# Causal attention: diagonal maxima by mask rows, all maxima in two halves of TensorE's array, a fixed cyclic order, three operand buffers

## The chip, the cores and the metric

The kernel runs on one core of a Trainium2 chip. Its engines are TensorE (PE in the profile; PEld is its weight loader), VectorE (DVE), ScalarE (ACT), GpSimdE (POOL) and SyncE, whose queue (SPq) issues nearly all DMAs. The metric is the device time of one execution in microseconds (us), as the median of several runs. Less is better.

## The reference

Two transformer blocks on `x` of shape (16, 1024, 256), in FP32. What matters here is the attention of the second block: 16 heads of 16 dimensions over 1024 positions, causal, with a linear position bias (ALiBi), for each of 16 batch entries. It is cut here to its core:

```python
q = (x @ q_w + q_b).reshape(Bx, Tx, NH, HD).transpose(0, 2, 1, 3)
kv = (x @ kv_w + kv_b).reshape(Bx, Tx, 2, NH, HD).transpose(2, 0, 3, 1, 4)
k, v = (kv[0], kv[1])
att = jnp.einsum('bhqd,bhkd->bhqk', q, k) * (1.0 / np.sqrt(HD))
att = att + build_alibi_bias(NH, Tx)[None]
att = jnp.where(causal[None, None], att, -jnp.inf)
att = jax.nn.softmax(att, axis=-1)
y = jnp.einsum('bhqk,bhkd->bhqd', att, v)
y = y.transpose(0, 2, 1, 3).reshape(Bx, Tx, Cx)
return y @ o_w + o_b
```

## The kernel before

Three stages follow each other. `prepare` sets up constants and small products (to about 152 us), `project` makes q, k, v and the feed-forward part in 32 steps and stores them to DRAM (to about 870 us), and `attend` does the attention (the rest). The change is in `attend`, with small additions to the other two.

`attend` works through 64 tasks `t` (`GROUPS`): batch entry `t // 4` and group `t % 4` of four heads. q and k are held as sums of three BF16 parts, and their products of parts stand in one contraction of up to 109 rows: three position rows, six products of 16 dimensions (`NSLOT`, 99 rows to `KA`), three rows that subtract the row maximum (to `KB`, 102), and seven mask rows (to `KM`, 109). For each task PE does:

- `max` (30 units, L1499 to L1508): q times k for the keys before the diagonal block, into one of three PSUM banks `t_a`, and DVE reduces each bank to row maxima (L1647);
- `diag` (8 units, L1510 to L1518): the 128 x 128 diagonal blocks of four heads into a bank of the ring `t_r`; ACT copies it to `t_near` (L1608), POOL masks later keys there (L1750), and DVE reduces two blocks at once (L1654);
- `join` (DVE) and `split` (POOL) make three BF16 parts of the maxima, `rows` (L1525) turns them on PE, `lift` (ACT, L1616) copies them out, and SP writes them to DRAM (L1461), waits until they have landed, and reads them back into rows of `t_q` (L1463);
- `exp` (38 pieces, L1542 to L1557): logits with the maximum already subtracted, into the ring of four banks; ACT takes the exponential into one of six slots of `t_prob` (L1599), and POOL zeroes later keys in diagonal blocks (L1744);
- `weigh` (12 quads, L1559 to L1573): probabilities times v in FP32, four heads side by side in column tiles of 32, into the bank `t_y`;
- `swap`, `invert`, `scale`, `back` on DVE (L1668 to L1688) turn and divide the result; `yhigh` (ACT) and `ylow` (POOL) split it, and for each fourth task PE does four units `out` (L1528 to L1540), which DVE adds to the residual (L1693).

The order of the instructions on each engine is fixed before the run. `plan()` (L1177) walks through time with given costs and picks, for PE, the unit of lowest rank whose inputs would be ready; the orders of the other engines follow. Operands `t_q`, `t_k`, `t_v` have four buffers, one for each group of heads; the 13 loads of task t + 4 are issued by SP after the last `weigh` of task t (L1465).

Of the kernel before, what the change touches and what calls it, by code (L numbers as in the profile page):

```python
# [11 lines left out]
P = 128  # L12
# [10 lines left out]
GH = 4  # L23
# [13 lines left out]
SUB = 16  # L37
EPS = 1e-5
# [3 lines left out]
class Chain:  # L42
# [5 lines left out]
    def __call__(self, ins):  # L48
        self.n += 1
        ins.then_inc(self.sem, 1)  # L50
        self.eng.wait_ge(self.sem, self.base + self.n)


def prepare(nc, a, scr):
# [8 lines left out]
    with ctx:  # L63
# [18 lines left out]
        keep(early, "t_v0", [P, QT, VPAD])  # L82
        blocks = keep(early, "t_blocks", [KM - KB, P])
        blockb = keep(early, "t_blockb", [KM - KB, P], BF16)
        for name in ("t_s_c0", "t_s_qkv0"):
            scr[name] = early.enter_context(nc.semaphore(name))
# [12 lines left out]
        ones = sb("p_ones", [P, P])  # L99

# [80 lines left out]
        s_wl, s_wh, s_blocks = sem("p_weights_in"), sem("p_w_hi_done"), sem("p_blocks")  # L181
# [53 lines left out]
        def _(pool):  # L235
# [29 lines left out]
            for it in range(ROUNDS):  # L265
                power(0, it)
                if it + 1 < ROUNDS:
                    power(1, it + 1)

# [391 lines left out]
def project(nc, a, scr):  # L661

    ctx = ExitStack()
    with ctx:  # L664
# [11 lines left out]
        q0, k0, v0, blockb = (scr["t_" + n] for n in ("q0", "k0", "v0", "blockb"))  # L676
        s_c0, s_qkv0 = scr["t_s_c0"], scr["t_s_qkv0"]
# [61 lines left out]
        def _(sp):  # L739
# [8 lines left out]
            def first_group():  # L748

                qs, ks = (scr[n].rearrange("s b (h d) t -> s b d h t", d=HD) for n in ("qs", "ks"))  # L750
                vs = scr["v"].rearrange("b (j p) (g c) -> b g p j c", p=P, g=NG)
                tiles = lambda t: t.rearrange("p (o n) -> p o n", o=1).to_broadcast([KM - KB, GH * QT, P])
                blocks = lambda t: t[KB:KM, :, :].rearrange("p h (i n) -> p (h i) n", n=P)
                sp.dma_start(q0[0:NPOS, :, :], a["q_pos"][:, 0:GH, :]).then_inc(s_c0, 16)
                sp.dma_start(k0[0:NPOS, :, :], a["k_pos"]).then_inc(s_c0, 16)
                sp.dma_start(k0[KA:KB, :, :], a["k_one"]).then_inc(s_c0, 16)
                sp.dma_start(blocks(q0), tiles(a["bmask"][SUB:P:SUB, :])).then_inc(s_c0, 16)
                sp.dma_start(blocks(k0), tiles(blockb[:, :])).then_inc(s_c0, 16)
                sp.wait_ge(s_q_out, 96)
                for n in range(2):  # L760
                    sp.wait_ge(s_k_out[n], 48)
                    sp.wait_ge(s_v_out[n], 16)
                for s in range(NSLOT):
                    at = NPOS + s * HD
                    sp.dma_start(q0[at:at + HD, :, :], qs[Q_PART[s], 0][:, 0:GH, :]).then_inc(s_qkv0, 16)
                    sp.dma_start(k0[at:at + HD, :, :], ks[K_PART[s], 0][:, 0:GH, :]).then_inc(s_qkv0, 16)
                sp.dma_start(v0[:, :, 0:GH * VW], vs[0, 0]).then_inc(s_qkv0, 16)
# [339 lines left out]
def max_units():  # L1107


    out = []  # L1110
    for i in range(1, QT):
        for k0 in range(0, i * P, 512):
            w = min(512, i * P - k0)
            out += [(i, k0, w, h, per_bank(w)) for h in range(0, GH, per_bank(w))]
    return out
# [10 lines left out]
A_BANKS, RING_BANKS, SLOTS = 3, 4, 6  # L1126
OUTS = 4
NSUB = KM - KB


class Planner:
# [5 lines left out]
    def __init__(self):  # L1137
        self.done, self.free = {}, dict(PE=0.0, ACT=0.0, DVE=0.0, POOL=0.0)
        self.order = {n: [] for n in ("PE", "ACT", "DVE", "POOL", "SP")}
        self.todo = {n: [] for n in ("ACT", "DVE", "POOL")}  # L1140
        self.row = {}
# [34 lines left out]

def plan():  # L1177


    lead, lag = 1.5, 0.12  # L1180
    pl = Planner()
    width = [KEY_QUADS[r][3] * per_bank(KEY_QUADS[r][3]) for r, h0 in PIECES]
    at = [sum(width[:x]) / sum(width) for x in range(NP_ + 1)]
    load = [n * w + 65 for i, k0, w, h, n in MAX_UNITS]
    way = [sum(load[:u]) / sum(load) for u in range(NU + 1)]
    mm = lambda w: 4 + 0.42 * w

    streams = {"max": [], "exp": [], "weigh": [], "out": [], "diag": []}
    for t in range(GROUPS):
        streams["max"] += [(t - lead + way[u], "max", t, u) for u in range(NU)] + [(t - lead + 1.12, "rows", t, 0)]  # L1190
        streams["diag"] += [(t - lead - 0.25 + 0.9 * i / QT, "diag", t, i) for i in range(QT)]
        streams["exp"] += [(t + at[x], "exp", t, x) for x in range(NP_)]
        streams["weigh"] += [(t + at[FIRST_PIECE[r // 2 * 2 + 2]] + lag, "weigh", t, r) for r in range(NQ)]
        if t % NG == NG - 1:
            streams["out"] += [(t + (1.0 if 2 * h < OUTS else 1.25) + 0.12 * h, "out", t // NG, h) for h in range(OUTS)]
    streams = {n: list(reversed(s)) for n, s in streams.items()}
    slot_freed, ring_freed = [], []

    def maxima_in(t):
        if all(("max", t, u) in pl.done for u in range(NU)) and all(("reduce", t, i) in pl.done for i in range(QT // 2)):  # L1200
            pl.give("DVE", max(pl.when("reduce", t, i) for i in range(QT // 2)), t - lead + 1, ("join", t, 0), 320,
                    lambda end: pl.give("POOL", end, t - lead + 1, ("split", t, 0), 1250))

    def selected(t, i, end):
        if i % 2 == 1:
            pl.give("DVE", end, t - lead + 0.5, ("reduce", t, i // 2), 1141, lambda end: maxima_in(t), "reduce")

    def weighted(t, c, end):
# [3 lines left out]
        def inverted(end):  # L1212
            pl.give("DVE", end, t + 0.5, ("scale", t, c), 370, scaled)
        def swapped(end):
            pl.give("DVE", end, t + 0.5, ("invert", t, c), 290, inverted)
        pl.give("DVE", end, t - 0.5, ("swap", t, c), 620, swapped)

    def turned(t, c, end):
# [3 lines left out]
        if t % NG == 1 and c == 0:  # L1222
            pl.order["SP"] += [("residual", t // NG, 0)]
            for x in range(OUTS):
                for z in range(2):
                    pl.give("POOL", end + 8000 + 3000 * (2 * x + z), t + 1.2 + 0.25 * x, ("shift", t // NG, 2 * x + z), 1300)

    def possible(kind, t, x):
        ready = 0.0
        if kind in ("max", "rows", "out") and len(slot_freed) >= A_BANKS:  # L1230
            ready = pl.when(*slot_freed[-A_BANKS])
        if kind in ("exp", "diag") and len(ring_freed) >= RING_BANKS:
            ready = pl.when(*ring_freed[-RING_BANKS])
        if kind in ("max", "diag") and x == 0:
            if t >= 2:
                ready = max(ready, pl.when("split", t - 2, 0))
            if t >= NG:
                ready = max(ready, pl.when("weighed", t - NG, NQ - 1) + 12000)
        if kind == "diag" and NG * t + x // 2 >= 4:
            n = QT // 2 * t + x // 2 - 2  # L1240
            ready = max(ready, pl.when("reduce", n // (QT // 2), n % (QT // 2)))
        if kind == "rows":
            ready = max(ready, pl.when("split", t, 0))
        if kind == "exp":
# [4 lines left out]
            if n >= 0:  # L1249
                ready = max(ready, pl.when("weighed", n // NQ, n % NQ) - 250)  # L1250
        if kind == "weigh":
            ready = max(ready, pl.when("masked", t, x), pl.when("masked", t, x // 2 * 2 + 1))
# [7 lines left out]
    now, tiled = 0.0, False  # L1260
    while any(streams.values()):
        pl.settle(now)
        heads = [s[-1] for s in streams.values() if s]
        ready = {e: possible(*e[1:]) for e in heads}
        able = [e for e in heads if ready[e] <= now]
        if not able:
            later = [z for z in ready.values() if z < pl.FAR / 2]
            later += [max(e[0], pl.free[n]) + 1 for n, todo in pl.todo.items() for e in todo]
            now = min(z for z in later if z > now)
            continue  # L1270
        stay = [e for e in able if tiled and e[1] == "weigh" and e[0] < min(able)[0] + 0.1]
        rank, kind, t, x = min(stay or able)
        streams["max" if kind == "rows" else kind].pop()
        pl.order["PE"].append((kind, t, x))
        if (kind == "weigh") != tiled:
            tiled, now = not tiled, now + 90
        if kind == "max":
            i, k0, w, h, n = MAX_UNITS[x]
            now += n * mm(w)
            slot_freed.append(("max", t, x))  # L1280
            pl.give("DVE", now + 165, rank, ("max", t, x), n * w * 1.04 + 66, lambda end, t=t: maxima_in(t), "slot")
        elif kind == "diag":
            now += GH * mm(P)
            ring_freed.append(("keep", t, x))
            def kept(end, t=t, x=x):
                pl.give("POOL", end, t - lead, ("future", t, x), 700, lambda end: selected(t, x, end), "future")
            pl.give("ACT", now + 165, rank, ("keep", t, x), 470, kept, "ring")
        elif kind == "rows":
            now += 80
            slot_freed.append(("lift", t, 0))  # L1290
            pl.give("ACT", now + 165, rank, ("lift", t, 0), 200, lambda end, t=t: pl.order["SP"].append(("lift", t, 0)))
# [13 lines left out]
        elif kind == "weigh":  # L1305
# [4 lines left out]
            if x == NQ - 1 and t + NG < GROUPS:  # L1310
                pl.order["SP"].append(("load", t, 0))
        elif kind == "out":
            now += 12 * 118
            slot_freed.append(("sum", t, x))
            last = lambda end, t=t: pl.order["SP"].append(("store", t, 0))
            pl.give("DVE", now + 165, rank, ("sum", t, x), 616, last if x == OUTS - 1 else None, "slot")
    pl.settle(pl.FAR)
    return pl.order


def attend(nc, a, scr, out):

    ctx = ExitStack()
    with ctx:
# [7 lines left out]
        blockb = scr["t_blockb"]  # L1332
# [527 lines left out]
```

## Time and profile before

| | |
|---|---|
| Median of 3 runs | 2729.24 us (2727.04 to 2734.53) |
| The profiled execution | 2729.97 us, its span 2727.9 us |
| Mean granted TensorE clock | 0.978 |
| Instructions | 57513 |
| Busy PE, DVE, ACT, POOL | 2598.3, 2321.1, 2059.8, 1373.4 us |

The page gives the busy time of each engine over the whole span. PE's ends are modelled, so that a PE that is busy nearly all the time may still wait; starts of instructions in the timeline tell more. A group of instructions in the view by line shows busy time, mean duration and the idle time before it. Durations of neighbours overlap by some tens of ns.

### The profile page before, as it was taken

The numbers are of one execution on the slowest core, as the hardware profiler recorded it, in microseconds if no ns is written. First come the engines' busy times: TensorE is split into PE (matmuls) and PEld (weight loads), VectorE is DVE, ScalarE is ACT, GpSimd is POOL, SyncE is SP. The second block draws the span as 40 slices with busy tenths as digits, with TensorE's granted clock in tenths as the row PEclk, the third lists the DMA queues.
The fourth block names the chain that finished last, engine by engine and source line by source line (L and its number), as shares of the span: only waits on it lengthen the run. The fifth ranks groups of instructions, "written<-read, shape, count | busy, mean of one in ns | idle before, by whom it ended". The sixth has DMA issues, their size and how long they took to land.

```text
span 2727.9 us, 57513 instructions
## 1 busy us (share of the span) xinstructions
PE 2598.3 (95%) x21670; PEld 1637.9 (60%) x21670; DVE 2321.1 (85%) x4175; ACT 2059.8 (76%) x3887; POOL 1373.4 (50%) x1768
## 2 busy tenths in 40 slices
PE   6779999999997999999999999999999999999998
PEld 4569989999996444545445454454544545455454
DVE  3468888888886998999989998899998999999993
ACT  2248878877884687888887887788887887887886
POOL 2235555555653365464654645546464464654644
PEclk9889999999998899999999999999999999999999
DMA  2015575545555646556474564655546556474540
GB/s 73 1 44 171 179 189 186 173 164 177 176 178 165 106 74 123 80 99 106 73 127 75 104 105 68 122 82 98 100 79 122 82 97 102 77 127 77 103 89 17
DMA packets 315172, 299.58 MB, mean 110 GB/s; under 512 B 97174, under 2 KB 265516, under 8 KB 314668
## 3 DMA queue, kind: packets, MB, share of 16 engines
q1 hardware_dynamic: 313344, 295.55, 50.9%
q8 instruction: 171, 2.80, 0.4%
q14 instruction: 105, 0.86, 0.1%
q10 hardware_dynamic: 1552, 0.36, 0.1%
HBM read 175.27 MB, written 120.06 MB: 108 GB/s over the span
## 4 chain that ended last, share of the span: by engine, by line
PE 54%; ACT 6%; DMA 5%; issue 1%; SPq 0%; DVE 0%; POOL 0%; POOLq 0%; ACTq 0%
PE t_y L1570 19%; PE t_r L1554 16%; PE t_a L1505 12%; ACT t_prob L1599 6%; DMA scr_m<-t_mrows 4%; PE t_a L1538 4%; PE t_r L1516 3%; DMA t_q<-scr_m 1%; DMA t_k<-t_blockb 0%; DVE t_mxc L1647 0%; ACT t_mrows L1616 0%; SPq L1411 0%; ACT t_near L1608 0%; SPq L1417 0%; POOL t_prob L1744 0%
## 5 line engine op out<-in xcount | busy, mean ns | idle before, releaser
L1599 ACT ACTIVATE t_prob<-t_r 128x512 f32<-128x512 f32 (+1 forms) x2432 | 1261.4, 599 | 289.5 <-PE t_r L1554 285.4
L1647 DVE TENSOR_REDUCE t_mxc<-t_a 128x1 f32<-128x512 f32 (+3 forms) x1920 | 1129.3, 643 | 105.4 <-PE t_a L1505 102.7
L1554 PE MATMUL t_r<-t_q,t_k 109*128 109x128 bf16 (+4 forms) x4608 | 831.7, 275 | 31.1 <-DMA t_q<-scr_m 20.9
L1505 PE MATMUL t_a<-t_k,t_q 99*128 99x512 bf16 (+3 forms) x2560 | 650.1, 320 | 1.5 <-DVE t_mxc L1647 1.0
L1750 POOL TENSOR_SCALAR_AFFINE_SELECT t_near<-t_near 128x512 f32<-128x512 f32 x512 | 332.7, 650 | 532.3 <-ACT t_near L1608 532.1
L1570 PE MATMUL t_y<-t_prob,t_v 128*32 128x512 f32 (+3 forms) x6144 | 588.0, 496 | 0.0
L1554 PEld LDWEIGHTS t_r<-t_q,t_k 102*128 102x128 bf16 (+1 forms) x4608 | 373.6, 98 | 342.9 <-ACT t_prob L1599 133.1
L1744 POOL TENSOR_SCALAR_AFFINE_SELECT t_prob<-t_prob 128x512 f32<-128x512 f32 x512 | 322.5, 637 | 276.9 <-ACT t_prob L1599 276.9
L1608 ACT COPY t_near<-t_r 128x512 f32<-128x512 f32 x512 | 307.5, 602 | 82.6 <-PE t_r L1516 65.6
L1505 PEld LDWEIGHTS t_a<-t_k,t_q 99*128 99x128 bf16 x2560 | 210.8, 98 | 228.5 <-DVE t_mxc L1647 155.0
L1570 PEld LDWEIGHTS t_y<-t_prob,t_v 128*32 128x32 f32 x6144 | 157.7, 109 | 257.3 <-issue 182.4
L1654 DVE TENSOR_REDUCE t_mxd<-t_near 128x8 f32<-128x1024 f32 x256 | 308.6, 1207 | 0.8 <-POOL t_near L1750 0.8
L1516 PE MATMUL t_r<-t_k,t_q 99*128 99x128 bf16 x2048 | 200.4, 222 | 19.2 <-PEq L664 8.9
L1085 POOL TENSOR_TENSOR j_part<-p_rest,j_part 128x1024 bf16<-128x1024 f32 x64 | 138.1, 2158 | 136.5 <-ACT j_part L902 136.5
L1516 PEld LDWEIGHTS t_r<-t_k,t_q 99*128 99x128 bf16 x2048 | 150.6, 99 | 85.0 <-ACT t_prob L1599 20.2
L826 PE MATMUL j_b<-j_x1s,p_w_hi 128*128 128x512 f32 x512 | 160.6, 395 | 1.7 <-DVE j_ffn L1041 1.7
L1055 POOL TENSOR_TENSOR j_rstd<-j_ve,j_neghalf 128x4 f32<-128x4 f32 x64 | 92.9, 1452 | 129.6 <-DVE j_ve L966 129.6
L1670 DVE STREAM_TRANSPOSE t_ysw<-t_y 128x512 f32<-128x512 f32 x128 | 90.8, 709 | 40.8 <-PE t_y L1570 40.6
L908 ACT CAST j_mixs<-p_mix 128x1024 fp32r<-128x1024 f32 x64 | 67.5, 1054 | 59.0 <-DVE p_mix L974 59.0
L1771 POOL TENSOR_TENSOR t_yl<-t_yT,t_yh 128x512 fp32r<-128x512 f32 x64 | 81.7, 1276 | 52.1 <-ACT t_yh L1623 52.1
L826 PEld LDWEIGHTS j_b<-j_x1s,p_w_hi 128*128 128x128 f32 x512 | 94.3, 189 | 21.0 <-issue 1.9
L819 PE MATMUL j_b<-p_w_hi,j_xT 128*128 128x256 f32 x512 | 99.4, 287 | 2.5 <-DVE j_xT L969 2.5
(199 smaller groups left out, 4129.2 us busy)
## 6 DMA issues: line engine op xcount, KB each, us to landing
t_q<-scr_q SPq DMA_DIRECT2D x384, 128.0 KB, 4.0
t_k<-scr_k SPq DMA_DIRECT2D x384, 128.0 KB, 6.6
scr_q<-j_part SPq DMA_DIRECT2D x96, 256.0 KB, 3.4
scr_k<-j_part SPq DMA_DIRECT2D x96, 256.0 KB, 2.5
scr_v<-j_v SPq DMA_DIRECT2D x32, 544.0 KB, 5.0
t_v<-scr_v SPq DMA_DIRECT2D x64, 272.0 KB, 8.1
p_x<-in_x SPq DMA_DIRECT2D x32, 512.0 KB, 4.3
scr_res<-j_x SPq DMA_DIRECT2D x32, 512.0 KB, 3.8
```

The lines of the kernel that those rows point to most:

```text
L826: mm = pe.matmul(bk[:, c * MS:(c + 1) * MS], weight[y][:, k, c * P:(c + 1) * P], src[x][:, k, :], start=(n == 0), stop=(n == len(TERMS) - 1))
L1085: pool.tensor_tensor(part[:, slot_of(n, m), 2, :, :], rest[:, n, :, :], part[:, slot_of(n, m), 1, :, :], ALU.subtract).then_inc(s_lo[n], 1)
L1505: mm = pe.matmul(abank[n % A_BANKS][:, x * w:(x + 1) * w], q_op[t % NG][0:KA, h0 + x, i * P:(i + 1) * P], k_op[t % NG][0:KA, h0 + x, k0:k0 ...
L1516: mm = pe.matmul(ring[n % RING_BANKS][:, h * P:(h + 1) * P], q_op[t % NG][0:KA, h, i * P:(i + 1) * P], k_op[t % NG][0:KA, h, i * P:(i + 1) ...
L1554: mm = pe.matmul(ring[n % RING_BANKS][:, s * w + lo:s * w + hi], k_op[g][0:deep, h0 + s, j * P:(j + 1) * P], q_op[g][0:deep, h0 + s, q0 + ...
L1570: mm = pe.matmul(ybank[32 * h:32 * h + 32, q0 - 512 * c:q0 - 512 * c + w], v[t % NG][:, j, h * VW:h * VW + 32], prob[:, (NQ * t + r) % SLO ...
L1599: nc.scalar.activation(prob[:, q % SLOTS, h0:h0 + m, 0:w], ring[n % RING_BANKS][:, 0:m * w].rearrange("p (h n) -> p h n", h=m), ACT.Exp).t ...
L1608: nc.scalar.copy(near[:, z % 2, i % 2, :, :], ring[n % RING_BANKS][:, :].rearrange("p (h n) -> p h n", h=GH)).then_inc(s_e, 1)
L1647: V.tensor_reduce(mxc[:, t % 2, k0 // 512, h0:h0 + m, i], abank[n % A_BANKS][:, 0:m * w].rearrange("p (h n) -> p h n", h=m), AX.X, ALU.max ...
L1654: V.tensor_reduce(mxd[:, t % 2, :, 2 * i:2 * i + 2].rearrange("p h i -> p i h"), near[:, z % 2, :, :, :], AX.X, ALU.max, negate=True).then ...
L1744: pool.affine_select(piece, piece, [[0, GH], [1, P]], ALU.is_ge, zero, base=0, channel_multiplier=-1).then_inc(s_mask, 1)
L1750: pool.affine_select(piece, piece, [[0, GH], [-1, P]], ALU.is_ge, never, base=0, channel_multiplier=1).then_inc(s_near, 1)
```

## The change

**Maxima.** `diag`, `keep`, `future` and `reduce` are gone. All maxima, the diagonal ones too, come from one kind of unit, 19 for a task. Of the nine products of parts only three are used (51 rows with the position rows, `NMAIN`), so that two heads fit into the halves of the array: one in the rows from 0, one in the rows from 64. On the diagonal 12 mask rows are added (63 rows, `NMAX`), whose values grow by powers of two, so that a later key gets a large negative number. A unit writes one bank for each half, into one of two slots of two banks each, and DVE reduces both banks with one instruction of 1024 or 768 elements. The operands for this are in tiles of their own, `t_qm` and `t_km`.

**PSUM.** Two slots of two banks (`A_SLOTS`) and a ring of three banks, for three banks and a ring of four.

**Order.** PE follows `CYCLE`, a table of 74 entries (kind, unit, lag of the task in periods) that repeats for each period. A period holds 19 `max`, 38 `exp`, 12 `weigh`, one `rows`, and those `out` that are due: 0, 0, 1 and 3 in four periods. The planner now only follows this order and derives those of the other engines. SP's order is by planned time, with the loads in three pieces and the new loads of keys in two.

**Buffers.** Three operand buffers rotate over tasks. Task t's maxima operands are freed after its last `max`, its other operands after its last `weigh`, and the loads of task t + 3 follow. The q positions are loaded for each task.

**Other.** `scale` moves from DVE to POOL, `join` is one instruction. `prepare` makes the mark rows on POOL (46 `memset`, 4 selects, 2 copies). In `project` the first group's loads grow from 18 to 38 DMAs.

The core of the diff:

```diff
 def max_units():
-    out = []
-    for i in range(1, QT):
-        for k0 in range(0, i * P, 512):
-            w = min(512, i * P - k0)
-            out += [(i, k0, w, h, per_bank(w)) for h in range(0, GH, per_bank(w))]
-    return out
+    units = [((0, 0, P, True), (4, 512, P, True)) for h in range(1)]
+    units += [((1, 0, 2 * P, True), (5, 512, 2 * P, True)) for h in range(2)]
+    units += [((i, k0, 3 * P, True),) for i, k0 in ((2, 0), (6, 512)) for h in range(2)]
+    units += [((i, k0, 4 * P, i * P < k0 + 512),) for i, k0 in ((3, 0), (4, 0), (5, 0), (6, 0), (7, 0), (7, 512)) for h in range(2)]
+    return [(pieces, range(2) if u == 0 else (1 - u % 2,)) for u, pieces in enumerate(units)]
-A_BANKS, RING_BANKS, SLOTS = 3, 4, 6
+A_SLOTS, RING_BANKS, SLOTS = 2, 3, 6
+BUFS = 3
+CYCLE = (
+    ("exp", 25, 9), ("exp", 26, 9), ("weigh", 2, 9), ("weigh", 3, 9), ("rows", 0, 8), ("exp", 27, 9),
+    ("exp", 28, 9), ("exp", 29, 9), ("max", 5, 7), ("max", 4, 7), ("weigh", 4, 9), ("weigh", 5, 9),
+    ("max", 10, 6), ("max", 12, 6), ("exp", 30, 9), ("exp", 31, 9), ("exp", 32, 9), ("weigh", 6, 9),
+    ("exp", 33, 9), ("exp", 34, 9), ("exp", 35, 9), ("max", 13, 6), ("max", 17, 6), ("exp", 36, 9),
+    ("exp", 37, 9), ("weigh", 7, 9), ("max", 18, 6), ("exp", 0, 8), ("exp", 1, 8), ("out", 1, 10), ("exp", 2, 8),
...
+    ("weigh", 1, 8), ("exp", 21, 8), ("out", 0, 9), ("exp", 22, 8), ("max", 14, 6), ("exp", 23, 8),
+    ("out", 3, 10), ("exp", 24, 8), ("max", 9, 6),
+)
+def load_maxima(eng, a, scr, q, k, t, done, e):
+    b, g = divmod(t, NG)
+    mine = slice(g * GH + e * GH // 2, g * GH + (e + 1) * GH // 2)
+    eng.dma_start(q[64 * e:64 * e + NPOS, :, :], a["q_pos"][:, mine, :]).then_inc(done, 16)
+    for op, src, parts in ((q, parts_of(scr, "qs"), Q_MAIN), (k, parts_of(scr, "ks"), K_MAIN)):
+        for n, s in enumerate(parts):
+            at = 64 * e + NPOS + n * HD
+            eng.dma_start(op[at:at + HD, :, :], src[s, b][:, mine, :]).then_inc(done, 16)
     # TensorE: largest(t, u, n)
-                for x in range(m):
-                    mm = pe.matmul(abank[n % A_BANKS][:, x * w:(x + 1) * w],
-                                   q_op[t % NG][0:KA, h0 + x, i * P:(i + 1) * P],
-                                   k_op[t % NG][0:KA, h0 + x, k0:k0 + w], start=True, stop=True)
+                for h in pair:
+                    for i, k0, w, near in pieces:
+                        far = w - P if near else w
+                        for depth, lo, hi in ((NMAIN, 0, far), (NMAX, far, w)):
+                            if lo < hi:
+                                for e in range(2):
+                                    mm = pe.matmul(abank[n % A_SLOTS][:, 512 * e + at + lo:512 * e + at + hi],
+                                                   q_max[t % BUFS][64 * e:64 * e + depth, h, i * P:(i + 1) * P],
+                                                   k_max[t % BUFS][64 * e:64 * e + depth, h, k0 + lo:k0 + hi],
+                                                   start=True, stop=True)
+                        at += w
     # SyncE
+                elif what == "load":
+                    sp.wait_ge(s_pv, NQ * (t + 1))
+                    n = t % BUFS
+                    load_operands(sp, a, scr, q_op[n], k_op[n], v[n], t + BUFS, s_qkv[n], x)
+                elif what == "keys":
+                    sp.wait_ge(s_a, last_max(t) + 1)
+                    n = t % BUFS
+                    load_maxima(sp, a, scr, q_max[n], k_max[n], t + BUFS, s_qk[n], x)
```

## Rows read from the trace of the kernel before

**Rows 1.** The page: busy time of each engine, share of the span, instructions.
```profile
PE 2598.3 (95%) x21670; PEld 1637.9 (60%) x21670; DVE 2321.1 (85%) x4175; ACT 2059.8 (76%) x3887; POOL 1373.4 (50%) x1768
```

**Rows 2.** Windows: four tasks in the attention stage.
```profile
core 0: us, PE busy (x) PEld busy (x) DVE busy (x) ACT busy (x) POOL busy (x), PEclk, DMA share, GB/s
1195.80:1309.30 113.50, 112.45 (x1037) 58.44 (x1035) 105.96 (x181) 94.09 (x197) 60.66 (x94) 1.00 0.56 98
```

**Rows 3.** Waits in the same four tasks: total us, times, longest.
```profile
PEld t_a L1505 <- DVE t_mxc L1647: 10.6, 18, 0.8
```

**Rows 4.** Start of the attention, and turnings of `ybank`: timeline, and by tile.
```profile
870.72 1.44 PE L1516 MATMUL t_r<-t_k,t_q 99*128 99x128 bf16 x12 [8.94 <-PEq L664]
...
940.01 0.70 DVE L1670 STREAM_TRANSPOSE t_ysw<-t_y 128x512 f32<-128x512 f32 x1
...
L1670 DVE STREAM_TRANSPOSE t_ysw<-t_y x101: 704/706/718, 1195.8 to 2611.8; 128x512 f32<-128x512 f32 x101
...
L1670 DVE STREAM_TRANSPOSE t_ysw<-t_y x128: 704/706/718, 919.6 to 2712.6; 128x512 f32<-128x512 f32 x128
```

**Rows 5.** Timeline of TensorE and its weight loader: start us, duration us, what.
```profile
1312.89 0.38 PE L1505 MATMUL t_a<-t_k,t_q 99*128 99x512 bf16 x1
1313.11 0.38 PE L1516 MATMUL t_r<-t_k,t_q 99*128 99x128 bf16 x4
1313.33 0.38 PE L1554 MATMUL t_r<-t_q,t_k 102*128 102x512 bf16 x1
...
1303.27 0.38 PE L1505 MATMUL t_a<-t_k,t_q 99*128 99x512 bf16 x1
1303.58 1.71 PE L1570 MATMUL t_y<-t_prob,t_v 128*32 128x512 f32 x16
1305.22 0.39 PE L1554 MATMUL t_r<-t_q,t_k 109*128 109x128 bf16 x2
...
1302.88 0.38 PEld L1516 LDWEIGHTS t_r<-t_k,t_q 99*128 99x128 bf16 x4
```

**Rows 6.** Chain of waits, 1200 to 1600 us: one unit of the output projection.
```profile
1361.92 1.63 PE t_a L1538 x12
```

**Rows 7.** Timeline of VectorE and ScalarE where instructions follow each other without waiting.
```profile
1299.56 3.68 DVE L1647 TENSOR_REDUCE t_mxc<-t_a 128x1 f32<-128x512 f32 x6 [0.31 <-PE t_a L1505]
...
882.19 2.34 DVE L1654 TENSOR_REDUCE t_mxd<-t_near 128x8 f32<-128x1024 f32 x2
...
2699.47 1.61 ACT L1599 ACTIVATE t_prob<-t_r 128x512 f32<-128x512 f32 x3
```

**Rows 8.** Groups of instructions in the same four tasks, by form.
```profile
L1608 ACT COPY t_near<-t_r 128x512 f32<-128x512 f32 x32 | 19.2, 601 | 3.9 <-PE t_r L1516 3.9
...
L1678 DVE TENSOR_TENSOR t_yn<-t_ysw,t_rec 128x256 f32<-128x256 f32 x8 | 4.6, 574 | 0.0
```

**Rows 9.** DMA queues in the same four tasks: busy tenths and GB/s in 40 slices.
```profile
DMA  7999900003799900000299992800008999992003
GB/s 144 138 138 134 99 14 12 0 0 89 144 148 149 129 17 9 0 0 0 60 180 142 146 131 88 288 20 0 0 6 175 164 162 160 334 349 63 9 0 92
```

**Rows 10.** The maxima's path through DRAM: timeline, then landings by tile (1200 to 2600 us).
```profile
1292.33 0.22 PE L1525 MATMUL t_a<-t_identb,t_mpart 128*96 128x128 bf16 x1
...
1293.83 0.33 SPq L1461 DMA_DIRECT2D scr_m<-t_mrows  x1
...
1300.51 0.26 SPq L1463 DMA_DIRECT2D t_q<-scr_m  x1
...
1302.37 0.39 PE L1554 MATMUL t_r<-t_q,t_k 109*128 109x128 bf16 x2 [0.32 <-DMA t_q<-scr_m]
...
DMA to landing us min/median/max: 1.4/3.6/8.7
```

**Rows 11.** Timeline of SyncE's queue: first and last of the first group's 18 loads.
```profile
353.35 0.38 SPq L754 DMA_DIRECT2D t_q<-in_q_pos  x1
...
363.12 0.43 SPq L767 DMA_DIRECT2D t_v<-scr_v  x1
```

## What the change does to the time: the prediction

> **What bounds the kernel now.** I read the page first, then the stretch of windows in the attention stage, then single PE rows. The page says PE is busy 95% of the span [rows 1], but that counts pipelined ends. In the attention stage one task (a group of four heads, 64 in all) takes 28.3 us: 50 tasks between the turning of `ybank` at 1195.8 and that at 2611.8 [rows 4], 1416/50. Four tasks hold PE busy 112.45 of 113.50 us, DVE 105.96, ACT 94.09 and POOL 60.66, at clock 1.00 and a DMA share of 0.56 [rows 2]. Per task: PE 28.1, DVE 26.5, ACT 23.5, POOL 15.2 us, DMA 15.9 us of all 16 engines.
>
> So I price PE by the distance between starts. A 512-column matmul takes 0.22 us, as do four of 128 [rows 5]: 0.42 ns a column and 3 or 4 ns each. Going into `weigh` costs something: the 512-wide one at 1303.27 should make room at 1303.48, but `weigh` starts at 1303.58: 0.10 us. The two quads then (512 and 384 wide, each column four times in FP32, 1.49 us) end in the next start 1.64 us later [rows 5]: 0.15 us more. A block of `weigh` thus costs 0.24 us beside its columns.
>
> Work per task before: far maxima 14336 columns in 40 matmuls, 6.1; diagonal 4096 in 32, 1.8; logits 18432 in 72, 8.0; `weigh` 4608 x 4 columns, 7.7, plus about 6.5 blocks x 0.24 = 1.6; output projection 12 matmuls at 0.12, 1.4 [rows 6]; `rows` 0.1. Sum 26.7. Against 28.3 that leaves 1.6 us of real waiting. DVE is the main reason: PE's weight loads for maxima waited for a DVE reduce 10.6 us in four tasks [rows 3]. The rest is the maxima's trip through DRAM, below.
>
> **The change on PE.** Maxima and diagonal are now one kind, two heads side by side in the halves of the array: 18432 columns become 9216 of time, 3.9 us, and 36 pairs add 10 ns each (two starts, as the four column tiles of `weigh` start 7 ns apart): 4.2 us for the 7.9 before, so 3.7 saved. No row of before shows two row halves. The ends for a pair: the time of one matmul (as in `weigh`, whose four column tiles share one stream) or of two (0.44 us for 512, nothing saved, +3.8). I take the first, for `weigh` is the nearest row.
>
> Against it stand layout changes. `CYCLE` changes between logits, maxima and `weigh` 38 times a period. `weigh` is entered 9 times: 9 x 0.24 = 2.2 (0.6 more than before). The other 20 changes are between maxima and logits and have no row; ends 0 and 0.12 each. I take 0.10, as for entering `weigh`: 2.0. Sum after: 4.2 + 8.0 + 7.7 + 2.2 + 2.0 + 1.4 + 0.1 = 25.6 us (23.6 to 26.0 by the ends of the layout price). So of 3.7 us saved 2.6 come back as layout changes. PE's work falls by only 1.1 us.
>
> **The other engines.** DVE reduces 18432 elements as before, but in 19 instructions for 34. Six back to back took 3.68 us and two of 1024 elements 2.34 [rows 7]: 0.60 for 512 and 1.13 for 1024, that is 0.065 fixed, so 15 fewer save 1.0. Two `scale` leave for POOL (4.6/4 = 1.15, [rows 8]) and one join goes (0.2): DVE 26.5 - 2.3 = 24.2 at most. At back-to-back rates the 19 reduces take 15 x 1.13 + 4 x 0.86 = 20.4, and the turnings of 0.7 [rows 4] and the small operations some 3.0 more: 23.4. That the source is two banks instead of one costs 0 to 0.07 a unit; I take 0. ACT loses eight copies, 19.2/4 = 4.8 us [rows 8]: 18.7. POOL loses eight of 16 selects and gains the two products, so it stays under its 15.2. Both have room, so these are worth nothing themselves, but the ring (three banks for four) then serves exponentials only, three at a time of about 0.5 us [rows 7], with 1.5 to 2.5 us of other PE work between triples in `CYCLE`: I cost it at nothing; if the triples came faster PE would wait 0.2 us at each.
>
> The output projection is not even: in four periods three hold 0, 0 and 1 of the four units and one holds 3. A period without it has 24.2 us of PE against 22.8 to 23.6 of DVE. That is tight with two slots (2.3 us of DVE work), but in `CYCLE` no stretch between two maxima, or two pairs of them, is longer than 2.3 us. I put 0.5 us of waiting for this (0 to 1.6).
>
> **DMA and SP.** Loads are issued after the last `weigh` of a task. At a full share they ran at 130 to 150 GB/s [rows 9]: 1.8 MB take 12.9 us. New are 12 loads of 64 KB and the positions, 0.82 MB: 5.6 us. With residual and store (3.1 MB in four tasks, at 330 GB/s, 2.4 us a task) the queue is busy 21.3 of about 26 us, 0.8 for 0.56. Slack for the loads themselves is more than a period, as three buffers with the keys apart still run ahead, so they cost nothing.
>
> The one short path is `rows` (place 4), `lift`, two DMAs, logits 0 (place 27). The work between these on PE is 7.0 us of columns and 11 layout changes, 8.4 us. The path in rows: transpose at 1292.33, first DMA at 1293.83, landed by 1300.51 when the second is issued, PE goes on at 1302.37 [rows 10]: 10.0 us, with 6.7 for the first landing. The median landing is 3.6 [rows 10]: 6.9 us, 1.5 to spare. PE stalls when the landing passes 5.1 us. Before `lift` stand, in the order of issue, the tail of the loads (from place 49, 12.9 us, ending 4 to 5 us into the next period, where `lift` comes at 2 us: landing 3 to 3.5), and in every fourth period the store (3.2 us): landing 6.5, a stall of 1.4, and one of about 2 in the next, whose loads started late behind the residual. I take 0.6 us a period on average (0 to 3).
>
> Period: 25.6 + 0.5 + 0.6 = 26.7 us; part of DVE's waiting goes under the DMA stall, so 26.5.
>
> **Once.** In the projection stage the first group gets 38 DMAs for 18. The 18 took from 353.35 to 363.55 [rows 11], about half a us each, while stores stood behind them: 20 more, +9 us (0 to 12; the cover would be store slack). The mark rows in `prepare` lie on an idle POOL: 0. Fill: from 870.7 to the turning at 940.0 it was 69.3 us [rows 4]. Now one period holds maxima of task 0 only (17 units, DVE's 18.7 us), the next 20.4, then 7 to logits 0, 13.5 to the end of that period, 16.5 to `weigh` 11 and 0.5: 76.6. Drain: the last three tasks took 70 us, the last turning at 2712.6 [rows 4] stands 15.3 before the end. Now no maxima there: 22 + 20 + 15.5 = 57.5, then 15.5.
>
> Sum: 870.7 + 9 + 76.6 + 60 x 26.5 + 57.5 + 15.5 = 2619.3 us of span. The profiled run took 2.1 us more than its span (2729.97) and lay 0.7 above the median: 2621 us.
>
> **Rivals.**
> (a) The order fits so well that no waiting is left: 60 x (25.6 - 26.5) = -54, so 2567; with the layout changes cheaper, DVE becomes the bound at 24.2: 2483. For: ACT and POOL have room. Against: 1.6 us of waits with DVE at 26.5 of 28.3.
> (b) Landing of the maxima late in each period, since the DMA share is 0.8: landings of 8 us as behind the residual give 10.0 + 1.3 - 8.4, some 2.9 us each period for the 0.6 in the sum: +138, 2759, slower. It decides from a landing of 7.5 us on in every period; at 6 us it gives 2639. For: 1.1 us is all that separates loads and `lift`. Against: the median 3.6.
> (c) The halves do not overlap as hoped. Full-array loads of 98 ns stand 55 ns apart under running matmuls (four in 0.38 us [rows 5]), so they are hidden. If in halves the loads of a pair are not hidden, 36 x 0.10 = 3.5 us more: 60 x 3.5 = +210, 2831, slower; if only the 20 pairs of 128 columns show 50 ns: +60, 2681. The Trainium skill, "TensorE: Matmul & The Clock Gate", Part 3 (what overlaps and what doesn't), says that a weight load overlaps a running matmul only where the row group differs; each half's next load has the same row group as its running matmul, so by that rule this rival is the outcome. The trace disagrees with it for the full array.
> (d) The change does not do what it says: each head pair serial, +3.8: 2849.
>
> **Chances.** Forecast 0.56 (2585 to 2665); (a) 0.15, of it 0.04 below 2540; (b) 0.16, a third of it slower than before; (c) 0.09, half of it slower; (d) 0.04. Range 2545 to 2715: it leaves out the deepest end of (a), the slower part of (b), most of (c), and (d). A measurement of this kernel can tell about 0.3%, 8 us. Faster by more: 0.84; within: 0.04; slower: 0.12.
>
> **What the new profile would show.** The distance between turnings of `ybank` four tasks apart: 106 us for 113.3. A 512-wide pair of maxima ends in a next start 0.22 (other kind: 0.32) us later; 0.44 is (d), 0.32 within a kind is (c). ACT busy near 18.7 and DVE near 24 a task. PE's wait for `t_q<-scr_m` at 0 in most periods and 1 to 2 us after a store; more means (b). In the projection stage one step of about 35 us near 360 for the 27 of before. Wrong would be above all the price of 20 layout changes without a row: 0.05 us more or less each is 60 us of time.

## The result and the profile after

| | before | after |
|---|---|---|
| Median | 2731.35 us (4 runs) | 2801.34 us (2799.70 to 2807.41, 4 runs) |
| Span of the profiled execution | 2727.9 us | 2799.1 us |
| Mean granted TensorE clock | 0.978 | 0.940 |
| Turning of `ybank`, mean distance over 60 tasks | 28.4 us | 29.3 us |

The change makes the kernel slower: ratio 1.0261, 95% interval 1.0239 to 1.0284. The forecast was 2621 us, range 2545 to 2715.

The page of the changed kernel, busy time of each engine, against [rows 1]:

```profile
PE 2536.6 (91%) x21670; PEld 1434.1 (51%) x21670; DVE 2201.9 (79%) x3022; ACT 1849.3 (66%) x3375; POOL 1123.3 (40%) x1436
```

Every engine does less than before and is idle for a larger share. So no engine became the bound; work waits for work. Four tasks in windows, against [rows 2], and then one place inside the stage (columns as there: length, busy time of PE, PEld, DVE, ACT, POOL, then clock, DMA share, GB/s):

```profile
1447.70:1565.00 117.30, 107.42 (x1022) 44.71 (x1018) 97.06 (x105) 79.25 (x161) 43.11 (x68) 0.95 0.64 121
...
1562.00:1574.00 12.00, 12.00 (x124) 4.88 (x124) 9.52 (x10) 9.42 (x19) 0.64 (x1) 1.00 0.72 216
1574.00:1579.00 5.00, 0.05 (x1) 0.00 (x0) 0.00 (x0) 0.09 (x1) 1.64 (x2) 0.88 1.09 233
1579.00:1591.00 12.00, 8.90 (x47) 2.53 (x49) 6.38 (x7) 6.01 (x13) 8.75 (x10) 0.50 0.48 85
```

From 1574 to 1579 TensorE, VectorE and ScalarE stand still and the DMA queues are full; GpSimd starts again at 1577.36. Afterwards TensorE works at 0.50 of its clock, its lower level of 1.2 GHz, for 12 us. This comes once in four tasks. The timeline of GpSimd, TensorE and ScalarE there (start, duration, what, idle time before and what ended it):

```profile
1565.50 0.64 POOL L1782 TENSOR_SCALAR_AFFINE_SELECT t_prob<-t_prob 128x512 f32<-128x512 f32 x1 [5.13 <-ACT t_prob L1655]
1577.36 1.26 POOL L1777 TENSOR_TENSOR t_res<-t_res,t_obias 128x512 f32<-128x512 f32 x1 [11.22 <-DMA t_o<-scr_ffn]
1578.57 1.81 POOL L1782 TENSOR_SCALAR_AFFINE_SELECT t_prob<-t_prob 128x512 f32<-128x512 f32 x3
1580.35 1.26 POOL L1777 TENSOR_TENSOR t_res<-t_res,t_o 128x512 f32<-128x512 f32 x1
1581.57 0.62 POOL L1803 TENSOR_TENSOR t_yn<-t_ysw,t_rec 128x256 f32<-128x256 f32 x1
...
1573.40 0.65 PE L1612 MATMUL t_r<-t_q,t_k 102*128 102x512 bf16 x2
1579.26 1.51 PE L1628 MATMUL t_y<-t_prob,t_v 128*32 128x384 f32 x8 [5.22 <-POOL t_prob L1782]
1580.70 0.61 PE L1612 MATMUL t_r<-t_q,t_k 102*128 102x512 bf16 x1
1584.14 0.61 PE L1612 MATMUL t_r<-t_q,t_k 102*128 102x512 bf16 x1 [2.83 <-ACT t_prob L1655]
...
1582.97 0.62 ACT L1671 CAST t_yh<-t_yT 128x512 fp32r<-128x512 f32 x1 [8.88 <-DVE t_yT L1729]
```

Each engine takes the instructions of its queue in order. GpSimd's next instruction was the first addition to the residual (`shift`, L1777), and the residual had not landed. Behind it in GpSimd's queue stood the masks of the probabilities (L1782), for which `weigh` on PE waited 5.22 us, and the product `scale` (L1803), for which DVE's turning, then ScalarE's `yhigh` and behind that the exponentials waited, and so PE a second time. Why the residual was late is in SyncE's queue:

```profile
1550.41 0.40 SPq L1543 DMA_DIRECT2D out<-t_o  x1
1552.05 2.37 SPq L1521 DMA_DIRECT2D scr_m<-t_mrows  x1
1560.09 0.26 SPq L1523 DMA_DIRECT2D t_q<-scr_m  x1
...
1566.99 0.38 SPq L1539 DMA_DIRECT2D t_res<-scr_res  x1
1567.41 0.58 SPq L1540 DMA_DIRECT2D t_o<-scr_ffn  x1
```

The maxima's trip through DRAM (L1521, L1523) took 8.0 us to its first landing (the time from the issue of a DMA until its data have arrived), behind the 1 MB store and the tail of the loads, and SyncE waits for it. The 14 key loads follow, and only then the residual, 15 us after the trip began; it landed 10 us later. In the kernel before, the residual had stood ahead of the trip. Over the whole stage the landings of the trip, by tile, against the 1.4/3.6/8.7 of [rows 10]:

```profile
DMA to landing us min/median/max: 1.4/5.9/8.5
```

### The profile page after: what moved, and what is told of

Read it like the earlier page. It is cut to its first block, busy times and chain, and to the rows that moved or that the text cites. A ratio compares the mean times of both kernels' runs of the same rounds, so it can differ in the third digit from the quotient of the medians.

```text
span 2799.1 us, 56352 instructions
## 1 busy us (share of the span) xinstructions
PE 2536.6 (91%) x21670; PEld 1434.1 (51%) x21670; DVE 2201.9 (79%) x3022; ACT 1849.3 (66%) x3375; POOL 1123.3 (40%) x1436
## 4 chain that ended last, share of the span: by engine, by line
PE 51%; DMA 7%; SPq 3%; POOL 3%; DVE 2%; issue 2%; ACT 1%; POOLq 0%; ACTq 0%; DVEq 0%
PE t_r L1612 19%; PE t_y L1628 18%; PE t_a L1570 10%; DMA t_o<-scr_ffn 5%; PE t_a L1595 3%; DMA scr_m<-t_mrows 2%; SPq L116 2%; DVE t_mxc L1705 2%; POOL t_res L1777 1%; POOL t_prob L1782 1%; ACT t_prob L1655 1%; PE t_a L1582 0%; DVE t_yT L1729 0%; POOL t_yn L1803 0%; SPq L112 0%
## 5 line engine op out<-in xcount | busy, mean ns | idle before, releaser
L1705 DVE TENSOR_REDUCE t_mxc<-t_a 128x2 f32<-128x1024 f32 (+3 forms) x1216 | 1358.4, 1160 | 134.1 <-PE t_a L1570 122.2
L1612 PE MATMUL t_r<-t_q,t_k 109*128 109x128 bf16 (+4 forms) x4608 | 733.0, 283 | 89.5 <-issue 44.8
L1628 PE MATMUL t_y<-t_prob,t_v 128*32 128x512 f32 (+3 forms) x6144 | 639.3, 513 | 61.4 <-POOL t_prob L1782 61.3
L1612 PEld LDWEIGHTS t_r<-t_q,t_k 102*128 102x128 bf16 (+1 forms) x4608 | 325.3, 99 | 521.7 <-ACT t_prob L1655 286.0
L1782 POOL TENSOR_SCALAR_AFFINE_SELECT t_prob<-t_prob 128x512 f32<-128x512 f32 x512 | 319.3, 637 | 415.3 <-ACT t_prob L1655 415.2
L1570 PE MATMUL t_a<-t_km,t_qm 63*128 63x128 bf16 (+4 forms) x4608 | 432.4, 284 | 30.3 <-DVE t_mxc L1705 21.5
L1570 PEld LDWEIGHTS t_a<-t_km,t_qm 51*128 51x128 bf16 (+1 forms) x4608 | 150.7, 95 | 416.6 <-DVE t_mxc L1705 204.7
L1803 POOL TENSOR_TENSOR t_yn<-t_ysw,t_rec 128x256 f32<-128x256 f32 x128 | 79.5, 621 | 439.3 <-PE t_a L1570 328.7
L1777 POOL TENSOR_TENSOR t_res<-t_res,t_obias 128x512 f32<-128x512 f32 x64 | 81.3, 1270 | 153.8 <-DMA t_o<-scr_ffn 153.8
L902 PE MATMUL j_b<-p_w_hi,j_x1s 128*128 128x256 f32 x512 | 96.8, 284 | 10.4 <-DVE p_rest L1071 10.4
L909 PE MATMUL j_b<-j_x1s,p_w_lo 128*128 128x512 f32 x256 | 100.6, 393 | 0.0
```

What stands on the lines that cost most here:

```text
L902: mm = pe.matmul(bk[:, t * D:(t + 1) * D], src[x][:, k, t * P:(t + 1) * P], weight[y][:, k, :], start=(n == 0), stop=(n == len(TERMS) - 1))
L909: mm = pe.matmul(bk[:, c * MS:(c + 1) * MS], weight[y][:, k, c * P:(c + 1) * P], src[x][:, k, :], start=(n == 0), stop=(n == len(TERMS) - 1))
L1570: mm = pe.matmul(abank[n % A_SLOTS][:, 512 * e + at + lo:512 * e + at + hi], q_max[t % BUFS][64 * e:64 * e + depth, h, i * P:(i + 1) * P], ...
L1612: mm = pe.matmul(ring[n % RING_BANKS][:, s * w + lo:s * w + hi], k_op[z][0:deep, h0 + s, j * P:(j + 1) * P], q_op[z][0:deep, h0 + s, q0 + ...
L1628: mm = pe.matmul(ybank[32 * h:32 * h + 32, q0 - 512 * c:q0 - 512 * c + w], v[t % BUFS][:, j, h * VW:h * VW + 32], prob[:, (NQ * t + r) % S ...
L1705: V.tensor_reduce(out, data, AX.X, ALU.max, negate=True).then_inc(s_au, 1)
```

## Experiments

Theory H: the instruction at the head of GpSimd's queue waits for the residual and holds up masks and product behind it. Theory T: the maxima's trip is slow because it stands behind the tail of the loads. Rival D: the queues carry too many bytes (DMA share 0.64 for 0.56), and order doesn't matter. All kernels but the seventh and eighth start from the changed kernel; an edit is in the planner unless said otherwise. "Period" is the mean distance of the turnings over 60 tasks in the profiled run. The time at the low clock is counted from 950 us to the end; before that, while the stage fills, every kernel has 35 to 60 us of it. The ratio is to the kernel before as timed beside each run (medians 2728.7 to 2734.2 us), so it is a better comparison across runs than the medians are.

| | median us | ratio to before (95%) | period us | low clock from 950 us on, us |
|---|---|---|---|---|
| before | 2731.4 | | 28.4 | 25 |
| after | 2801.3 | 1.026 (1.024 to 1.028) | 29.3 | 209 |
| e1_shift_late | 2689.9 | 0.985 (0.982 to 0.988) | 27.5 | 81 |
| e2_store_later | 2795.0 | 1.022 (1.018 to 1.026) | 29.3 | 227 |
| e3_both | 2687.1 | 0.984 (0.982 to 0.987) | 27.5 | 70 |
| e4_scale_dve | 2762.8 | 1.011 (1.008 to 1.014) | 28.6 | 152 |
| e5_loads_after_trip | 2610.0 | 0.957 (0.955 to 0.958) | 26.3 | 15 |
| e6_spread | 2593.5 | 0.951 (0.949 to 0.952) | 25.9 | 5 |
| e7_before_residual | 2756.4 | 1.010 (1.008 to 1.012) | 28.9 | 46 |
| e8_before_both | 2697.7 | 0.989 (0.987 to 0.990) | 27.9 | 11 |
| e9_loads_only | 2723.9 | 0.997 (0.995 to 0.998) | 28.0 | 152 |

### e1: the additions later on GpSimd

```diff
-            pl.give("POOL", end + 8000 + 3000 * n, NG * b + 2.2 + 0.12 * n, ("shift", b, n), 1300)
+            pl.give("POOL", end + 24000 + 3000 * n, NG * b + 2.2 + 0.12 * n, ("shift", b, n), 1300)
```

> Only the order on GpSimd changes: the eight additions to the residual of each batch entry stand 16 us later in its queue; every DMA, and the order on TensorE, stay. Theory H (head of line): in the changed kernel GpSimd waits up to 11 us for the residual's DMA once in four tasks, with masks and the scaling behind it, and TensorE stands still for about 5.2 + 3.2 us. That goes: 15 x 8.4 = 126 us less than 2801, 2675 us (2660 to 2700), and no TensorE wait for the masked probabilities over 1 us. Rival D (the DMA queues are overloaded, and everything that depends on them is late): nothing moves, 2795 to 2805 us.

Measured 2689.9 us, 111 less than the changed kernel and 1.5% under the kernel before, with every DMA and TensorE's order as they were. The wait of PE for masks is gone from the list of waits. H holds, D falls as the cause of this part. The 111 us are more than the 70 that the kernel had lost against before, and they are net: in the changed kernel the next trip started after the stall, when the queues had run empty, and landed after 1.4 us; without the stall it lands after 7.7 (medians).

### e2: the store after the trip

```diff
-                pl.issue.append((end, "store", t, 0))
+                pl.issue.append((end + 3000, "store", t, 0))
```

> Only the order on SyncE's queue changes: the 1 MB store of a batch entry is issued after the maxima's trip through DRAM and the first half of the keys instead of before them. Theory H: the trip's first landing in that task falls from about 8 to 3 to 5 us and TensorE's wait of 2.2 us for it goes, 15 x 2.2 = 33 us; and as SyncE is free some 3 us earlier, the residual lands up to 3 us earlier and the stall on GpSimd shrinks by up to that: 2720 to 2770 us. Rival D (total load on the queues counts, not its order): 2795 to 2805 us.

Measured 2795.0 us: a miss. The trip of that task did get faster (landing 8.0 to 5.5 us), but what SyncE gained there it lost again on the store, now behind the trip, and on the wait for its landing, since store and residual use the same tile `t_o`: the residual was issued 15.0 us after the trip's start in both kernels. GpSimd, though, came to its addition earlier, 12.0 us after the trip's start for 14.7, and so waited longer (medians of eleven). The waits in the stage, of this kernel from 1300 to 2600 us (total, times, longest):

```profile
POOL t_res L1777 <- DMA t_o<-scr_ffn: 137.3, 11, 13.5
...
PE t_y L1628 <- POOL t_prob L1782: 71.1, 11, 7.5
```

In the changed kernel the same two are

```profile
POOL t_res L1777 <- DMA t_o<-scr_ffn: 110.4, 11, 11.2
...
PE t_y L1628 <- POOL t_prob L1782: 42.7, 11, 5.2
```

TensorE's waits for the trip (in the list `PE t_r` with "issue") fell from 33.1 to 11.8 us, 2 us in four tasks; its wait for the masks took that back, 71.1 - 42.7 = 28 us in 11 times.

### e3: both

The two diffs above together.

> Both changes of order together. Theory H: the stalls are separate, so 2801 - 126 - 33 = 2642 us (2625 to 2665), below the kernel before by about 3%. A period of four tasks takes 110 to 111 us for 117. If the two hide each other's cover, it is no faster than the later additions alone (2675).

Measured 2687.1 us, no better than e1 and over the expected 2625 to 2665. The trip behind the store fell from 8 to 5.5 us, but the next task's trip rose from 7.7 us to 9 to 13: residual and loads now go out right before it (the residual 9.6 us ahead in the task read, 13.3 in e1). A wait had been handed from one task's trip to the next's. That pointed to the order of the loads as a whole, not to the store; e5 tests it.

### e4: the product back on VectorE

`scale` is given to "DVE" at 370 ns in place of "POOL" at 720, and its code moves with it.

> The division product goes back from GpSimd to VectorE, as in the kernel before; nothing else. Theory H: of the two chains behind the waiting addition one goes (product, turning, ScalarE's copy, exponentials: the 3.2 us wait of TensorE for a free ring bank), the masks' 5.2 us stay: 15 x 3.2 = 48 us less. VectorE gets 0.8 us more a task, of which at most half shows, 64 x 0.4 = 26 us. 2750 to 2785 us. If instead the move of the product had nothing to do with it: 2801 to 2830 us.

Measured 2762.8 us, 38 less. GpSimd still waited for the residual and PE for the masks (51.3 us in 11 times), and ScalarE's wait for the turning fell from 117.4 to 43.7 us. So having `scale` on an engine "with room" cost 38 us net in the kernel whose GpSimd queue was blocked. What the move is worth with the queue free was not run.

### e5: the loads of k behind the trip

```diff
-                pl.issue += [(now + 3000 * z, "load", t, z) for z in range(LOAD_PIECES)]
+                pl.issue += [(now + (0, 17000, 3000)[z], "load", t, z) for z in range(LOAD_PIECES)]
```

on top of e1.

> On top of the later additions (2690 us): of each task's loads the six of k (768 KB) are issued after the next maxima's trip and key loads instead of before them, so that the queue has run empty when the trip starts. The same bytes are moved. Theory T (what is left of TensorE's waits, 1.1 us a period for logits 0, is the trip standing behind the tail of the loads): the landings of the maxima rows fall from 5 to 8 us to 1.5 to 4 in the tasks without a store, and 0.6 to 1.0 us a period go: 2630 to 2655 us. Rival D (with a DMA share of 0.6 to 0.8 the trip is slow wherever it stands): landings stay over 5 us and the time within 5 us of 2690.

Measured 2610.0 us, 80 less than e1, a larger gain than expected, at the same bytes. Landings of the trip, by tile, in e1 and then in e5:

```profile
DMA to landing us min/median/max: 4.5/6.9/9.1
```

```profile
DMA to landing us min/median/max: 1.7/3.7/8.2
```

T holds and D falls: with the same bytes, and at a higher rate as the kernel is faster, the trip takes half as long if it doesn't stand behind the loads. Only in the task after the residual it still takes 6 to 8 us, although 1.5 to 4 had been expected there too.

### e6: store and residual spread out as well

On top of e5: the store 3 us later, as in e2; the residual's two loads in two periods; the additions 8 us later; and `t_o` alone waits for the store's landing.

```diff
-        pl.issue.append((end, "residual", b, 0))
+        pl.issue += [(end, "residual", b, 0), (end + 22000, "residual", b, 1)]
...
-            pl.give("POOL", end + 24000 + 3000 * n, NG * b + 2.2 + 0.12 * n, ("shift", b, n), 1300)
+            pl.give("POOL", end + 32000 + 3000 * n, NG * b + 2.2 + 0.12 * n, ("shift", b, n), 1300)
...
```

> On top of that: the store after the trip, the two residual loads in two periods (each after the key loads) and the additions on GpSimd 8 us later again. Theory T: no trip has more than a load's tail before it, landings under 4 us in all tasks, no TensorE wait over 1 us in the steady state, TensorE never at the low clock there: a period of 25.6 to 26.0 us, 2590 to 2620 us. Rival D: over 2650 us.

Measured 2593.5 us, 4.9% under the kernel before and 7.4% under the changed one. Four tasks of it, in windows:

```profile
1477.30:1581.00 103.70, 103.70 (x1015) 44.15 (x1014) 96.07 (x105) 78.76 (x160) 43.13 (x68) 1.00 0.69 138
```

PE is never idle, at full clock, and the DMA queues carry 138 GB/s at a share of 0.69, more than in the changed kernel (121 at 0.64). The median landing is

```profile
DMA to landing us min/median/max: 1.4/2.1/5.3
```

Two tasks in four still have landings of 2 to 5 us, where under 4 had been expected in all; no single gap between matmuls in the steady state is over 0.3 us.

### e7 and e8: the cause put into the kernel before

In the kernel before, the residual's loads are held back until the next trip is issued (e7); in e8 the additions stand 12 us later too.

```diff
-            pl.order["SP"] += [("residual", t // NG, 0)]
+            pl.held = [("residual", t // NG, 0)]
...
+    def lifted(t):
+        pl.order["SP"] += [("lift", t, 0)] + pl.held
+        pl.held = []
...
```

> The kernel before, with the cause put into it: SyncE issues the two residual loads after the maxima's trip instead of before it; GpSimd's queue stays as it is, and its first addition to the residual stands some 7 us after that trip's start. Theory H: the residual now lands after the addition is reached, GpSimd waits 4 to 8 us once in four tasks with the masks behind it, and TensorE stands; the trip itself gets faster (2 us once in four tasks, and 3.4 us of the low clock once in a while, go). 2735 to 2790 us, and TensorE waits for the masked probabilities appear. If the head of the line on GpSimd were harmless, the faster trip alone would give 2695 to 2705 us.

Measured 2756.4 us, slower than before by 1.0% although the trip that had stood behind the residual got faster (7 to 9 us, now 1.5 to 3). Only SyncE's order differs from the kernel before. The waits from 1195 to 2600 us, first of before, then of e7:

```profile
POOL t_res L1739 <- DMA t_o<-scr_ffn: 14.5, 11, 2.2
PEld t_y L1570 <- POOL t_prob L1744: 10.1, 34, 0.4
```

```profile
POOL t_res L1745 <- DMA t_o<-scr_ffn: 61.3, 13, 5.6
PEld t_y L1576 <- POOL t_prob L1750: 57.6, 50, 4.3
PE t_y L1576 <- POOL t_prob L1750: 32.9, 13, 3.4
```

> As the last, with GpSimd's additions to the residual 12 us later. Theory H: the cause is out again, and the faster trip is left: 0.45 us a period, 2695 to 2710 us. If the later additions crowd what comes after (the planner's own periods do not change, 27.6 us), it stays at 2730.

Measured 2697.7 us, 1.1% under before, and GpSimd's wait for the residual and TensorE's for the masks are gone from the list. So the wait can be put into the kernel before by the place of two loads in SyncE's queue, and in both kernels it goes with the place of eight additions in GpSimd's. The 59 us between e7 and e8 are not the additions' alone, though: the planner of this kernel picks TensorE's order itself and answered with another one at 627 of 5760 places. In e1 the orders of TensorE and SyncE were those of the changed kernel.

### e9: the loads of k alone

The diff of e5 on the changed kernel, the additions where they were.

> The changed kernel with only the loads of k behind the next trip (GpSimd's additions where they were). With the additions out of the way this was worth 80 us (2690 to 2610). Theory H + T (two separate waits): the trip's waits go here too, 2801 - 80 = 2721 us; as SyncE gets past the shorter trip some 2 us earlier, the residual lands earlier and GpSimd's stall may shrink by 1 to 2 us in four tasks, 15 to 30 us more: 2690 to 2725 us. Rival (the two are one cause, the residual's lateness being all the trip's): GpSimd's wait falls under 3 us and the time reaches 2610 to 2640 us.

Measured 2723.9 us, 77 less than the changed kernel (80 by the ratios); GpSimd still waited for the residual 92.8 us in 11 times from 1300 to 2500 us, and TensorE 26.7 us for the masks. Alone the two edits give 111 and 77, together 191: two separate waits.

## Why the prediction was wrong

The sum was 2619.3 us of span; 2799.1 were measured. By its own terms:

| term | predicted | measured | difference |
|---|---|---|---|
| start of the attention | 879.7 | 878.2 | -1.5 |
| fill to the first task's second turning | 76.6 | 81.0 | +4.4 |
| 60 periods | 26.5 each | 29.28 each | +167 |
| last three tasks | 57.5 | 67.9 | +10.4 |
| drain | 15.5 | 15.2 | -0.3 |

The rows for start and period, against [rows 4]:

```profile
878.21 0.61 PE L1570 MATMUL t_a<-t_km,t_qm 51*128 51x512 bf16 x2 [8.80 <-PEq L755]
...
L1718 DVE STREAM_TRANSPOSE t_ysw<-t_y x121: 703/706/718, 959.2 to 2716.0; 128x512 f32<-128x512 f32 x121
```

**PE's work: right.** 25.6 us a period was the price; in e6, where nothing else is late, a period takes 25.9. That leaves 0.3 us for the waiting between neighbours, for which 0.5 was set. The parts, from the changed kernel's timeline of PE:

```profile
1593.29 0.60 PE L1570 MATMUL t_a<-t_km,t_qm 51*128 51x512 bf16 x4
1593.83 0.73 PE L1612 MATMUL t_r<-t_q,t_k 109*128 109x128 bf16 x6
...
1569.90 0.63 PE L1570 MATMUL t_a<-t_km,t_qm 51*128 51x128 bf16 x16
1570.46 0.70 PE L1612 MATMUL t_r<-t_q,t_k 102*128 102x512 bf16 x2
```

Two pairs of 512 columns and a change of layout take 0.54 us, that is 2 x 0.22 + 0.10; eight pairs of 128 and the change take 0.56, that is 8 x 0.057 + 0.10. So a pair costs what one matmul costs, rival (d) is out, and the layout change without a row costs the 0.10 that was taken for it. The weight loads of the halves, 94 ns each, are hidden even at 128 columns: rival (c) is out too. By the Trainium skill, "TensorE: Matmul & The Clock Gate", Part 3 (what overlaps and what doesn't), each pair would have shown its load, by estimate 8 x 0.094 = 0.8 us more for the eight; in the halves, as in the full array, the trace disagrees.

**The other engines: right in size.** DVE 96.07/4 = 24.0 us a task in e6 for 23.4 to 24.2, ACT 19.7 for 18.7 (the copies were priced by their own 19.2 us in four tasks, but they had overlapped with neighbours, and ACT's busy time fell by 14.8, from 94.09 to 79.25), POOL 10.8, under its 15.2. The DMA terms, 12.9 + 5.6 + 2.4, add up to 20.9 us and not to 21.3; nothing hangs on that.

**The step that failed: "Both have room, so these are worth nothing".** GpSimd has room on average, 10.8 of 29.3 us, and I priced its queue by that. But `shift` waits for a DMA and stands in the same queue as the masks, and the change moved both ends of that wait: the residual's load goes to SyncE's queue behind a store, a trip and 14 key loads (the planner's lines for this, `residual(t + 1, end + 6000)` and `end + 8000 + 3000 * n`, were not weighed at all), and `scale` came into the queue behind it. In the kernel before, the same wait was 14.5 us in 11 times, and the list has no wait of TensorE's matmuls for a mask. Priced by e1: 29.28 - 27.45 = 1.8 us a period, 111 us in all, for which the sum had 0.

**The step mis-sized: the trip.** I gave it 0.6 us a period, with landings of 3 to 3.5 us and 6.5 behind the store. Measured were 5.4, 6.8 and 8.0 in three tasks of four, and 1.4 in the one after the long wait (medians); in e1, without that wait, all four are 5.2 to 7.9. Priced by e5 and e6: 1.2 + 0.4 = 1.6 us. The mechanism and its condition (a stall from a landing of 5.1 us on) were those of rival (b), and its cause was named ("1.1 us is all that separates loads and `lift`"). That condition held: the landings of e1 are on average 1.7 us over 5.1, against the 1.6 priced. What was wrong are the landings. The tail of the loads was laid out with 12.9 us of DMA from its place in `CYCLE`, pushed back only behind the residual; that each late trip holds back the keys, and these the next loads, fits the order in SyncE's queue but was not tested by itself. The sum 25.9 + 1.8 + 1.6 gives the measured 29.3; it must, as the terms are the steps from the changed kernel over e1 and e5 to e6. That they are separate is what e9 shows.

**What both terms carry with them** is the clock. After each long wait of PE the granted clock was 0.50 for 3 to 14 us: from 950 us on 209 us in all, for 25 before. By e1 the blocked queue cost 7.4 us in four tasks (111/15), and the two waits shown above are 5.2 + 2.8 = 8.0 us by themselves. Behind them 8.90 us of busy TensorE at half the clock stand for about 4.5 us more, by estimate. So what the low clock added is not separated from what PE caught up later, and stays open. The Trainium skill, "TensorE: Matmul & The Clock Gate", Part 1, has it that the throttled state is the default and activity releases it; the trace agrees, in that the granted clock was 0.50 after the long waits of PE and 1.00 throughout the four tasks of e6 without one.

**First group and fill: right.** One step of the projection took 34.5 us for 26.8 before (forecast 35), and 7.5 us were added for 9. The fill took 81.0 us for 76.6, although the granted clock was 0.50 up to 936 us, 58 of the 81 (39 of 69.3 before); the price of the first two periods was DVE's, which was busy 76.1 of the 81. The last three tasks took 10.4 us more, of which 5.4 are one more long wait (28.4 us for 23.0 in e5); the other 5 stand in e5 and e6 as well and are not explained.

Of the rivals' slower side only (b) was near, with 2759 us; the cause that decided, a queue's head, was on no list.

## What to carry to other kernels

An engine's queue is priced by its heads, not by its busy time: for each instruction on it that waits for a DMA, ask what stands behind it and who needs that, even if the engine is idle 60% of the time. A short DMA that all wait for should be issued when the queue has run empty; moving the loads of k behind it, 0.77 of 1.83 MB a task, was worth 80 us at the same bytes. And when a plan is made with assumed times, compare its order with the chip's at the slowest transfer: here the residual was issued 16.6 us after the store where the plan had 6, and moving eight instructions turned a loss of 2.6% into a gain of 1.5%, and all the edits of e6 together into one of 4.9%.

## What the runs showed of the hardware

Two heads in the halves of the array, 51 or 63 rows each, run at the pace of one: starts of a pair lay 3 to 4 ns apart, and pairs of 128 columns some 57 ns apart with their weight loads of 94 ns hidden. A change between the full array and halves cost 0.095 to 0.10 us, as did one into the four column tiles of `weigh` (0.095). A reduce over two PSUM banks (1024 elements) took 1.22 us, as one of 1024 elements from SBUF had (1.21). And where a small DMA stands in the order of issue decides its time: 24 KB took 8.0 us behind a 1 MB store and the tail of the loads, and 1.4 us in the task where the queues had run empty.
